# A 64-image fusion layer on one core: GpSimd's step order changed (guesses in two parts, scatters spread, image affine earlier), with swaps on TensorE, ScalarE and VectorE

## What is computed

```
h = layernorm(patchify(x) @ W + b, cls token, positions) * gamma + beta   # 37 image tokens
h = concat(h, txt)                                                        # 165 tokens, width 256, 64 batches
scores = q @ k.T * scale;  top 49 of 165 per row;  softmax over those;  @ v   # 16 heads
h = h + attention(layernorm(h)) @ W_out + b_out
x = layernorm(h)
logits -> top 8 of 64 experts, at most 128 tokens an expert, in token order
h = h + sum over experts (silu(x Wg) * (x Wu)) Wd * weight + shared expert (silu * up) @ down
```

## Time and profile before

| | |
|---|---|
| median of three runs | 3077.92 us |
| profiled execution, its own time | 3077.82 us |
| its span, first to last instruction | 3076.1 us |
| busy: PE / DVE / ACT / POOL | 2360.4 / 2486.5 / 2480.2 / 2181.0 us |
| mean granted TensorE clock | 0.882 |
| last 426 us (experts): ACT busy 96.1, DVE busy 193.3, POOL 247.5 us | |

### The profile page before, as it was taken

How to read it: one execution, slowest core, us unless ns; L and a number is a source line. 1 busy time by engine, 2 the same in 40 slices (tenths; PEclk the granted TensorE clock), 3 DMA queues, 4 the chain that set the end, 5 groups by cost and what they waited for, 6 DMA issues and landing times.

```text
span 3076.1 us, 74618 instructions
## 1 busy us (share of the span) xinstructions
PE 2360.4 (77%) x17233; PEld 2007.1 (65%) x17233; DVE 2486.5 (81%) x12929; ACT 2480.2 (81%) x11201; POOL 2181.0 (71%) x4319
## 2 busy tenths in 40 slices
PE   5677877778787778777887787787878787764887
PEld 4566666666676666666666676676667676544776
DVE  1798889888888899988989888988899888842444
ACT  3999999999999999989999899998999989811111
POOL 3457777777777777777777777777777777645665
PEclk7799988988999989988899889988888889867998
DMA  2011011010110110101101101001010100006886
GB/s 66 10 30 24 25 27 29 25 30 23 28 25 23 29 30 25 30 23 24 27 25 29 30 25 27 25 22 28 25 30 23 29 18 24 19 16 159 220 222 143
DMA packets 203389, 130.07 MB, mean 42 GB/s; under 512 B 101776, under 2 KB 194444, under 8 KB 202924
## 3 DMA queue, kind: packets, MB, share of 16 engines
q1 hardware_dynamic: 168064, 105.38, 12.7%
q0 software_dynamic: 34368, 19.34, 3.9%
q10 hardware_dynamic: 492, 0.45, 0.1%
HBM read 77.63 MB, written 34.09 MB: 36 GB/s over the span
## 4 chain that ended last, share of the span: by engine, by line
ACT 47%; PE 14%; POOL 13%; issue 11%; DVE 6%; DMA 4%; another core or an unknown queue 2%; ACTq 0%; POOLq 0%; SPq 0%; DVEq 0%
ACT JK L877 23%; ACT E L865 9%; PE bank L1766 4%; ACT PTT L901 4%; DMA out<-E,X 3%; ACT JL L890 3%; POOL slot_token L683 3%; ACT PTI L906 2%; PE bank L1688 2%; PE bank L1691 2%; POOL X L662 2%; POOL out L793 2%; ACT KT L843 1%; PE bank L1757 1%
## 5 line engine op out<-in xcount | busy, mean ns | idle before, releaser
L877 ACT ACTIVATE JK<-S,thr 128x165 f32<-128x165 f32 x2688 | 1120.5, 422 | 14.5 <-POOL thr L624 7.2
L683 POOL DMA_INDIRECT slot_token<-TOKI,SLOT x512 | 533.5, 1042 | 221.8 <-issue 204.4
L662 POOL TENSOR_SCALAR X<-S,nt 128x165 f32<-128x165 f32 x1344 | 582.7, 452 | 75.4 <-DVE LIST L1158 66.1
L865 ACT ACTIVATE E<-bank,nb 128x165 f32<-128x165 f32 x1344 | 508.5, 391 | 10.8 <-DVE S L1083 9.6
L877 ACT ACTIVATION_READ_ACCUMULATOR JK<-S,thr 128x1 f32 x2688 | 510.7, 190 | 0.0
L1277 DVE SCALAR_TENSOR_TENSOR PR<-S,TV,E 128x165 f32<-128x165 f32 x1344 | 480.1, 405 | 0.2
L1083 DVE TENSOR_SCALAR_CACHE_REDUCE S<-bank 128x165 f32<-128x165 f32 x1344 | 364.5, 320 | 86.9 <-PE bank L1691 47.4
L1705 PE MATMUL bank<-IDENT,PR 128*128 128x128 f32 x1344 | 222.2, 283 | 230.3 <-issue 116.1
L1158 DVE MAX8 LIST<-X 128x8 f32<-128x165 f32 x1344 | 351.3, 317 | 8.1 <-DVE X L1148 1.8
L1705 PEld LDWEIGHTS bank<-IDENT,PR 128*128 128x128 f32 x1344 | 154.8, 145 | 284.6 <-issue 163.2
L1688 PE MATMUL bank<-KZ,QA 128*128 128x165 f32 x1408 | 280.8, 346 | 45.6 <-ACT E L865 19.0
(11 more groups left out here) (211 smaller groups left out, 6358.3 us busy)
## 6 DMA issues: line engine op xcount, KB each, us to landing
S<-in_w_gate SPq DMA_DIRECT2D x64, 192.0 KB
S<-in_w_up SPq DMA_DIRECT2D x64, 192.0 KB
E<-in_w_down SPq DMA_DIRECT2D x64, 192.0 KB
RD<-inverses SPq DMA_DIRECT2D x128, 82.5 KB
x_rows<-X SPq DMA_DIRECT2D x64, 160.0 KB
H<-in_txt SPq DMA_DIRECT2D x64, 128.0 KB
QA<-QT SPq DMA_DIRECT2D x512, 10.3 KB
QB<-QT SPq DMA_DIRECT2D x512, 10.3 KB
```

Source lines behind the costliest of these rows:

```text
L662: last = pool.tensor_scalar(X[n % DEEP][:, t % GROUP, :], S[r % 2][:, t, :], nt[r % 2][:, t:t + 1], DOWN, ALU.add, ALU.mult)
L683: pool.indirect_dma_start(slot_token, bass.IndirectOffsetOnAxis(SLOT[r % 2][:, 0, k:k + 1], 0), TOKI[r % 2][:, :], None, bounds_check=SLOT ...
L865: act.activation(E[r % 2][:, t, :], chunks(bS[g % 3], GROUP, T)[:, t % GROUP, :], ACT.Exp, bias=nb[:, t:t + 1], scale=-1.0, accum_out=sz[: ...
L877: act.activation(JK[:, t % 4, :], S[r % 2][:, t, :], ACT.Sign, bias=(t0, t1)[n][:, t:t + 1], scale=-1.0, accum_out=(c0, c1)[n][:, t:t + 1] ...
```

## The change

GpSimd's `guess` is cut in two: `guess` (the two operations on nb alone, which now wait for `take` and not for `exps`) and `guess2` (the other three). In GpSimd's iteration: `front_scale` goes ahead of `apart` 3; the first packed scatter goes between the first guess and `apart` 5; `front_affine` moves from ahead of `refine2` to behind `apart` 6; `front_center` and the first `refine` go ahead of the second guess; only one of the `back_slots` scatters is left ahead of it, and three follow it; `refine2` of tiles 0 to 8 goes ahead of the last two scatters. On TensorE, `back_glu` goes ahead of `scores(i, 3)` and `front_v` ahead of `transposes(i-2, 4)`. On ScalarE, `front_v` (VZ) goes ahead of `transposed(i-2, 4)`. On VectorE, `take(i, r, 3)` goes behind `back_glu`, `back_glu2` and `front_norm2`, and `front_embed2` goes from behind `threshold` to behind `side(i-1, 0)`. The counts in the waits on s_up are adapted. The number of instructions of every kind stays the same.

```diff
@@ -611,11 +611,17 @@
             def guess(i, r, half):
 
                 lo, hi = HALVES[half]
-                n = UP * i + 5 * half
-                pool.wait_ge(s_exp, EX_N * i + hi)
+                pool.wait_ge(s_take, NT * i + hi)
                 gated()
                 pool.tensor_scalar(v0[:, lo:hi], nb[:, lo:hi], -GUESS[3], GUESS[1], ALU.mult, ALU.add).then_inc(s_up, 1)
                 pool.tensor_scalar(v1[:, lo:hi], nb[:, lo:hi], -GUESS[2], GUESS[0], ALU.mult, ALU.add).then_inc(s_up, 1)
+
+            def guess2(i, r, half):
+
+                lo, hi = HALVES[half]
+                n = UP * i + 7 * half
+                pool.wait_ge(s_exp, EX_N * i + hi)
+                gated()
                 pool.wait_ge(s_up, n + 1)
                 pool.tensor_tensor(v0[:, lo:hi], v0[:, lo:hi], sz[:, lo:hi], ALU.mult).then_inc(s_up, 1)
                 pool.wait_ge(s_up, n + 3)
@@ -630,7 +636,7 @@
                 gated()
                 pool.tensor_scalar(u0[:, lo:hi], c0[:, lo:hi], 0.5 * SLOPE, 1.0 + SLOPE * (T / 2 - AIM),
                                    ALU.mult, ALU.add).then_inc(s_up, 1)
-                pool.wait_ge(s_up, UP * i + 11 + 2 * half)
+                pool.wait_ge(s_up, UP * i + (6, 13)[half])
                 pool.tensor_tensor(t1[:, lo:hi], t0[:, lo:hi], u0[:, lo:hi], ALU.mult).then_inc(s_up, 1)
 
             def refine2(i, r, half):
@@ -685,6 +691,8 @@
                                             oob_is_err=False).then_inc(s_slot[r % 2], 16)
 
             def pack_tokens(n):
+                if n == 0:
+                    pool.wait_ge(s_empty, 16)
                 if n >= 2:
                     pool.wait_ge(s_packed[n % 2], PS * (n // 2))
                 if n >= 1:
@@ -726,45 +734,46 @@
                     front_scale2(i + 1)
                 if has(i - 1):
                     apart(i - 1, (r - 1) % RING, 2)
+                if trio(i + 4):
+                    front_scale((i + 4) // PACKED)
+                if has(i - 1):
                     apart(i - 1, (r - 1) % RING, 3)
                     apart(i - 1, (r - 1) % RING, 4)
                 if has(i + 1):
                     front_bias(i + 1, (r + 1) % RING)
                 if has(i):
                     guess(i, r, 0)
+                    guess2(i, r, 0)
+                if True:
+                    packed(i, 0)
                 if has(i - 1):
                     apart(i - 1, (r - 1) % RING, 5)
+                    apart(i - 1, (r - 1) % RING, 6)
                 if trio(i + 4):
-                    front_scale((i + 4) // PACKED)
-                if has(i - 1):
-                    apart(i - 1, (r - 1) % RING, 6)
+                    front_affine((i + 4) // PACKED)
                 if has(i - 4):
                     back_tokens(i - 4, r)
                 if True:
-                    packed(i, 0)
                     packed(i, 1)
+                    packed(i, 2)
                 if has(i - 4):
-                    back_slots(i - 4, r, 0, 2)
-                if True:
-                    packed(i, 2)
-                if has(i):
-                    guess(i, r, 1)
-                if has(i - 4):
-                    back_slots(i - 4, r, 2, 4)
+                    back_slots(i - 4, r, 0, 1)
                 if has(i + 1):
                     front_center(i + 1)
                 if has(i):
                     refine(i, r, 0)
+                    guess(i, r, 1)
+                    guess2(i, r, 1)
+                if has(i - 4):
+                    back_slots(i - 4, r, 1, 4)
+                if has(i):
+                    refine(i, r, 1)
                 if has(i - 4):
                     back_slots(i - 4, r, 4, 6)
                 if has(i):
-                    refine(i, r, 1)
+                    refine2(i, r, 0)
                 if has(i - 4):
                     back_slots(i - 4, r, 6, 8)
-                if trio(i + 4):
-                    front_affine((i + 4) // PACKED)
-                if has(i):
-                    refine2(i, r, 0)
                 if has(i - 2):
                     back_scale(i - 2)
                 if has(i):
@@ -857,7 +866,7 @@
 
                 if g == 0:
 
-                    ahead(act, s_up, UP * (i - 1) + 10, i - 1 if known(i) else i)
+                    ahead(act, s_up, UP * (i - 1) + 12, i - 1 if known(i) else i)
                     ahead(act, s_prob, NT * (i - 1), i - 2 if known(i) else i)
                 act.wait_ge(s_take, NT * i + GROUP * (g + 1))
                 for t in range(GROUP * g, GROUP * (g + 1)):
@@ -870,7 +879,7 @@
                 for t in tiles:
                     if t in (0, AHEAD):
                         half = t // AHEAD
-                        act.wait_ge(s_up, UP * i + (5 + 5 * half, 12 + 2 * half)[n])
+                        act.wait_ge(s_up, UP * i + (5 + 7 * half, 7 + 7 * half)[n])
                     if t % 2 == 0 and (n or t or not known(i) or i):
 
                         act.wait_ge(s_cnt, CN * i + NT * n + max(t - 2, 0))
@@ -974,11 +983,10 @@
                 if has(i):
                     exps(i, r, 5)
                     exps(i, r, 6)
-                if has(i - 2):
-                    transposed(i - 2, 4)
                 if has(i + 1):
                     front_v(i + 1, (r + 1) % RING)
                 if has(i - 2):
+                    transposed(i - 2, 4)
                     transposed(i - 2, 5)
                 if has(i):
                     count(i, r, 0, range(AHEAD, NT))
@@ -1074,7 +1082,7 @@
                 if g == 0:
 
                     ahead(dve, s_exp, EX_N * i, i - 1)
-                    ahead(dve, s_up, UP * (i - 1) + 10, i - 1 if known(i) else i)
+                    ahead(dve, s_up, UP * (i - 1) + 12, i - 1 if known(i) else i)
                     ahead(dve, s_xp, NG * (i - 1), i - 2)
 
                     ahead(dve, s_prob, NT * (i - 1), i - 2 if known(i) else i)
@@ -1418,18 +1426,19 @@
                 if trio(i + 4):
                     front_embed_stats((i + 4) // PACKED)
                     front_embed_aggr((i + 4) // PACKED)
-                if has(i):
-                    take(i, r, 3)
                 if has(i - 3):
                     back_glu(i - 3)
                     back_glu2(i - 3)
                 if has(i + 1):
                     front_norm2(i + 1, (r + 1) % RING)
                 if has(i):
+                    take(i, r, 3)
                     take(i, r, 4)
                 if has(i - 1):
                     third_count(i - 1, 3)
                     side(i - 1, 0)
+                if trio(i + 4):
+                    front_embed2((i + 4) // PACKED)
                 if has(i - 3):
                     back_out(i - 3, (r - 3) % RING)
                 if has(i - 1):
@@ -1495,8 +1504,6 @@
                     nearest(i - 1, 6)
                     candidates(i - 1)
                     threshold(i - 1)
-                if trio(i + 4):
-                    front_embed2((i + 4) // PACKED)
                 if has(i - 1):
                     threshold2(i - 1)
                     threshold3(i - 1, (r - 1) % RING)
@@ -1805,11 +1812,10 @@
                     transposes(i - 2, 0)
                 if has(i - 3):
                     back_xt(i - 3, (r - 3) % RING)
+                if has(i - 3):
+                    back_glu(i - 3)
                 if has(i):
                     scores(i, 3)
-                if has(i - 3):
-                    back_glu(i - 3)
-                if has(i):
                     scores(i, 4)
                 if has(i - 3):
                     back_down(i - 3)
@@ -1834,11 +1840,10 @@
                     scores(i, 6)
                 if has(i + 1):
                     front_qk(i + 1, 1)
-                if has(i - 2):
-                    transposes(i - 2, 4)
                 if has(i + 1):
                     front_v(i + 1)
                 if has(i - 2):
+                    transposes(i - 2, 4)
                     transposes(i - 2, 5)
                     values(i - 2, (r - 2) % RING)
                 if has(i + 1):
```

2 lines of the change are left out of this document (1 added, 1 removed).

## The result

The changed kernel takes 3186.03 us (median of 4 runs, 3181.60 to 3189.29), the kernel before, in the same place and time, 3077.56 us (3074.23 to 3079.49): a ratio of 1.0353, 95% interval 1.0335 to 1.0371. That is 108 us more, where 10 were forecast, and outside the range of 3018 to 3118.

The account below looks back on a forecast made before the run. ScalarE's chain was taken to set the loop's pace. A trio's three iterations were given +1.6, +0.2 and -1.3, together +0.5 us; 21 trios made +10 us on 3077.8, so 3088 us, range 3018 to 3118 us.

Parts of the forecast that it names:

- Second guess in A: GpSimd, iterations with the affine: the second guess comes late and the Sign passes wait for it, +1.6 us.
- The swap of VZ and PTT: ScalarE before the last PTT copy: with VZ ahead of both copies, +0.6 us in iterations without the affine.
- Brs: End of GpSimd's iteration, ahead of back_scale: the X2T wait in a trio's second iteration shrinks by about half, -0.3 us.
- back_glu, +0.1: TensorE, back_glu ahead of scores 3: ScalarE's wait moves from TH to XT, +0.1 us in iterations without the affine.
- VZ's late signal in C: ScalarE before VZ, third iteration of a trio: TensorE's completion signal no longer comes late, so the 1.97 us wait goes.
- The first: Faster rival: front_xt does not follow TensorE's queue length, so the gain at TH stays; 3021 us, chance 20%.
- the second: Faster rival: GpSimd has unseen slack, so the second guess is not late in iterations with the affine; 3054 us, chance 17%.
- the third: Slower rival: TensorE's signal to VZ stays late in a trio's third iteration; 3130 us, chance 13%.
- the fourth: Rival of no change: all shifts in the loop stay under cover; 3078 us, chance 5%.

Follow-up runs that it names:

- e10: The changed kernel with front_affine behind the fifth and sixth slot scatters again, ahead of refine2: 3194.6 us, ratio 1.0417 to the kernel before.
- e8: The changed kernel with the front_v swap undone on TensorE alone, ScalarE's kept: 3132.3 us, ratio 1.0210 to the kernel before.
- e1: The changed kernel with front_v behind transposes 4 again, on TensorE and ScalarE: 3131.8 us, ratio 1.0155 to the kernel before.
- e3: The changed kernel with the last two slot scatters ahead of refine2 again: 3122.8 us, ratio 1.0123 to the kernel before.
- e4: The changed kernel with the front_v swap, the back_glu swap and the late last two scatters all undone: 3062.3 us, ratio 0.9918; again 3057.3 us, 1.0068.

## Why the prediction was wrong

By kind, A took 2.4 us more than before, B 2.0 and C 1.0 more, where +1.6, +0.2 and -1.3 were forecast.

- **Second guess in A, +1.6: right as a mechanism.** T0 + 28.5 for 28.1, A 42.4 us for 42.0, in half of the A iterations; in the other half A takes 43.8 us and more, by the waits of the other terms at XT and X2T. What it was set against was no fixed thing: in its second profile, without VZ's waits, the kernel before waits for the guess there. And e10 shows that undoing it by moving the affine gains nothing.
- **The swap of VZ and PTT, +0.6 in B and C: the step that failed first.** It costed ScalarE's half of the swap, a round trip that is there (0.64 us) and that costs little or nothing at the end (e8). TensorE's half was not costed at all: what `front_v` waits for, and what had filled that wait. TensorE now stands still for 2.26 us where e1 has 1.56, `front_v` and transposes 4 take 4.36 us where e1 has 2.66, and both lie ahead of PTT: 54 us in all.
- **Brs, -0.3: wrong sign.** The term set one affine against two scatters in A and left out B and C, where nothing was removed. Placing the two scatters behind the waiting `refine2` cost 0.9 us at brs in the mean of the iterations and 63 us. Nor was there any slack for it: "ScalarE hardly waits otherwise" passed over the 19.8 us at X2T in the profile of before.
- **back_glu, +0.1: mechanism right, size wrong.** TH's wait did move to XT, and the time was said to be up to 0.5 us later; it was 35 us, 0.55 us an iteration. The slow end of the stated bound was the true one, and it left out that `back_glu` would now run at the low clock.
- **VZ's late signal in C, -2.0: nothing to gain.** The signal is on time in the changed kernel, as the step said, but the step took for a property of the kernel what one profile showed and the next two did not, and where it is missing ScalarE waits for the guess instead (25.7 us in the stretch). C took 1.0 us more and not 1.3 less.
- **The rivals.** The first (TensorE is not the limit) fell with XT's waits, the second with A's late guess, the third with VZ on time, the fourth (nothing reaches the end) with all of them. None had an engine made idle by the change, and so the range ended at 3118. The forecast's own range is also added up wrong: A between +1.0 and +2.2 and B and C each off by 0.3 give 3063 to 3113, not 3068 to 3106; the measured time is outside of either.

The three terms that cost the time (the swap, brs, `back_glu`) have one form: a step was moved past another engine's wait, and the prediction asked who waits for the moved step, but not what had been done during the wait.

## What to carry to other kernels

When two steps change places in a queue, look at which of them waits, and for what: the other one was the filler of that wait. On TensorE the price was paid twice here, by the time that it stands and by the clock behind it. When a queue is full, as GpSimd's here, a step moved off one deadline lands on the next; price both, and keep the last producer of the next iteration's first input (here brs) right behind what it depends on. A wait whose releaser the profile cannot name, and that holds one term of a sum, is worth a second profile.

## What the runs showed of the hardware

- TensorE's granted clock fell behind a pause of 2.26 us: 1.00 in it, 0.60 in the 2.6 us after it and 0.61 in the 1.7 us after that; the same 12 matmuls of `front_v` took 2.60 us and, in e1 with a pause of 1.56 us and transposes ahead of them, 1.60. The length of the last pause alone does not tell it: `back_glu` ran at 0.59 behind pauses of 1.27 and 0.54 us with 0.68 us of transposes between them.
- One program's time differed by 1.7% between sets (medians 3030 to 3083 us), with the changed kernel at 3181 and 3186, and the ratio of the same two kernels was 1.035 and 1.047. The chip's number does not tell it: three sets on record under the same number have before at 3030, 3034 and 3071 us. The mean granted clock was 0.881 over the seven runs at 3083 and 0.895 over the 22 at 3030, but the changed kernel had 0.877 at 3186 and 0.854 at 3181: the cause is open.
- An indirect DMA of GpSimd behind another starts 0.30 us after it, behind arithmetic mostly 0.59 to 0.71 us (0.38 once in the A shown): scatters are cheapest in one run.
- Once in nine iterations GpSimd idled 2.9 us ahead of a scatter behind arithmetic, in the kernel before and the changed one; with the last four scatters in one run (e3, e4) it did not. The reason is open.
